# Returned rows of the second choices loaded from ScalarE's queue, those of the first choices from the sync engine

## The reference

```
x = x + _L0_ffn_ref(_layernorm(x), ...)      # top 2 of 8, silu gate
x = x + _L1_xattn_ref(ctx, ctx, _layernorm(x), mask, ...)
x = x + _L1_ffn_ref(_layernorm(x), ...)
x = x + _L2_xattn_ref(_layernorm(x), ctx, ...)
x = x + _L2_ffn_ref(_layernorm(x), ...)      # top 2 of 8, gelu
x = x + _L3_xattn_ref(_layernorm(x), ctx, ctx, ...)
x = x + _L3_ffn_ref(_layernorm(x), ...)      # top 2 of 8, relu
...
top_vals, top_idx = top_k(gate_logits, 2)
w = softmax(top_vals)
out = sum over both choices of w * expert(x)
```

## Time and profile before

| | us |
|---|---|
| median of 3 runs | 1276.0 |
| lowest and highest | 1274.1, 1277.46 |
| span of the profiled execution | 1241.1 |
| busy PE, DVE, ACT, POOL in it | 1028.2, 756.0, 658.9, 670.2 |

### The profile page before, as it was taken

One profiled execution on the slowest core, in us unless ns is written; L12 is line 12 of the kernel. 1 busy time (PEld: TensorE's weight loads), 2 busy tenths in 40 slices (PEclk: granted clock), 3 DMA queues, 4 the chain that ended last, 5 costly groups with the idle time before them and its releaser, 6 DMA issues.

```text
span 1241.1 us, 22522 instructions
## 1 busy us (share of the span) xinstructions
PE 1028.2 (83%) x6547; PEld 793.3 (64%) x6547; DVE 756.0 (61%) x2570; ACT 658.9 (53%) x2366; POOL 670.2 (54%) x1163
## 2 busy tenths in 40 slices
PE   3984999847899977986999998397699999966993
PEld 3874788734555547774677765386467776645993
DVE  4367254587878776247676687532776676754443
ACT  2225233337888952446887875243387888831321
POOL 5122456546666745257655565647475555655452
PEclk9775899977999995998999999599789999975998
DMA  3422446684920021420000000166300000014566
GB/s 60 4 27 89 131 155 208 202 145 164 389 84 2 2 69 35 136 78 1 19 1 18 18 2 18 41 178 186 96 18 2 1 1 2 2 35 124 172 203 196
DMA packets 132377, 102.82 MB, mean 83 GB/s; under 512 B 34651, under 2 KB 113939, under 8 KB 132256
## 3 DMA queue, kind: packets, MB, share of 16 engines
q1 hardware_dynamic: 121360, 82.38, 24.1%
q0 software_dynamic: 8448, 17.20, 4.2%
q10 hardware_dynamic: 2448, 1.80, 0.6%
HBM read 64.98 MB, written 36.36 MB: 82 GB/s over the span
## 4 chain that ended last, share of the span: by engine, by line
PE 53%; DVE 18%; issue 8%; POOL 8%; ACT 7%; DMA 5%; SPq 1%; DVEq 0%; ACTq 0%; POOLq 0%
PE ps L2645 5%; PE ps L2826 4%; PE ps L2647 4%; PE ps L2646 4%; PE ps L2840 4%; PE ps L2705 3%; ACT ex L1377 3%; DMA xr<-xr_d,src_i 2%; PE ps L2720 2%; POOL yq_d L884 2%; PE ps L2854 2%; POOL pp L1050 2%; PE ps L3318 2%; PE ps L3137 2%; ACT ex L1263 2%
## 5 line engine op out<-in xcount | busy, mean ns | idle before, releaser
L1050 POOL TENSOR_TENSOR pp<-ex,rc 128x256 f32<-128x256 f32 x384 | 236.1, 615 | 202.9 <-DVE rc L2178 144.9
L1263 ACT ACTIVATE ex<-ps,nmx 128x154 f32<-128x154 f32 x512 | 193.9, 391 | 70.5 <-DVE nmx L2173 69.2
L2173 DVE TENSOR_REDUCE nmx<-ps 128x2 f32<-128x308 f32 x256 | 119.4, 469 | 62.3 <-PE ps L2647 61.9
L884 POOL DMA_INDIRECT yq_d<-yq,ids_q x78 | 74.7, 957 | 75.4 <-DVE yq L1908 56.4
L2826 PEld LDWEIGHTS ps<-ident,pp 128*128 128x128 f32 x640 | 74.0, 142 | 57.5 <-POOL pp L1051 49.9
L1377 ACT ACTIVATE ex<-ps,nmx 128x154 f32<-128x154 f32 x256 | 97.4, 393 | 22.9 <-DVE nmx L2038 22.5
L2645 PE MATMUL ps<-kp,q_s 128*128 128x308 f32 x256 | 96.5, 377 | 15.1 <-ACT ex L1263 8.1
L1051 POOL TENSOR_TENSOR pp<-ex,rc 128x52 f32<-128x52 f32 x384 | 105.9, 276 | 0.0
L1263 ACT ACTIVATION_READ_ACCUMULATOR ex<-ps,nmx 128x1 f32 x512 | 105.0, 205 | 0.0
L2826 PE MATMUL ps<-ident,pp 128*128 128x128 f32 x640 | 100.5, 281 | 4.7 <-POOL pp L1051 4.7
L854 POOL TENSOR_TENSOR ln_r<-ln_v,mhalf 128x4 f32<-128x4 f32 x32 | 34.5, 1079 | 88.3 <-DVE ln_v L1659 76.8
(11 more groups left out here) (441 smaller groups left out, 2806.4 us busy)
## 6 DMA issues: line engine op xcount, KB each, us to landing
w_r<-in_L_ffn_W SPq DMA_DIRECT2D x69, 256.0 KB, 3.5
xq_d<-blankq SPq DMA_DIRECT2D x4, 4160.0 KB, 24.5
w_q<-in_L_ffn_W SPq DMA_DIRECT2D x46, 256.0 KB, 3.4
w_q<-in_L_ffn_w SPq DMA_DIRECT2D x46, 128.0 KB, 2.7
xq<-xq_d SPq DMA_DIRECT2D x22, 130.0 KB, 2.2
w_s<-in_L_ffn_W SPq DMA_DIRECT2D x8, 256.0 KB, 7.0
w_e<-in_L_ffn_W SPq DMA_DIRECT2D x8, 256.0 KB, 4.9
acc<-yq_d SPq DMA_DIRECT2D x8, 256.0 KB, 4.5
```

The source lines that it names most:

```text
L884: pool.indirect_dma_start(yq_d[:, :], bass.IndirectOffsetOnAxis(ap=ids_q[:, c:c + 1], axis=0), yq[k % NY][:, h, :], None).then_inc(q_out[k ...
L1050: pool.tensor_tensor(pp[st % 2][:, m % 4, 2 * j:2 * j + 2, :], w[:, :, 0:P], r.broadcast_to([P, 2, P]), ALU.mult)
L1263: ins = act.activation(ex[:, tt % NEX, j, :], ps[:, tt % 3, j * SK:(j + 1) * SK], ACT.Exp, bias=nmx8[:, tt % 8, j:j + 1], accum_out=sm8[:, ...
L2173: dve.tensor_reduce(nmx8[:, tt % 8, :], ps[:, tt % 3, 0:2 * SK].rearrange("p (h s) -> p h s", h=2), AX.X, ALU.max, negate=True).then_inc(n ...
```

## The change

The loads of the first choices stay on SP. Those of the second choices are issued by ScalarE: at entry A behind its four key copies; at entry B between products 7 and 8 of `preps(1, ...)`; at entry C after the last run of layer 3. ScalarE waits for the same semaphores of the scatters ahead of them. Each consumer waits for the same counts as before.

```diff
@@ region(l), SP @@
                 for b in range(B):
-                    for c, into in enumerate((acc, y_other)):
-                        sp.dma_start(into[:, bsl(b)].rearrange("p (k d) -> p k d", k=TB),
-                                     yq_d[c * B * S + b * S:c * B * S + (b + 1) * S, :].rearrange("(k p) d -> p k d", p=P)).then_inc(y_in[b], 16)
+                    sp.dma_start(acc[:, bsl(b)].rearrange("p (k d) -> p k d", k=TB), yq_d[b * S:(b + 1) * S, :].rearrange("(k p) d -> p k d", p=P)).then_inc(y_in[b], 16)
@@ sorted_runs(), SP @@
                 for b in range(B):
-                    for c, into in enumerate((acc, y_second)):
-                        sp.dma_start(into[:, bsl(b)].rearrange("p (k d) -> p k d", k=TB),
-                                     yr_d[FRONT + c * B * S + b * S:FRONT + c * B * S + (b + 1) * S, :].rearrange("(k p) d -> p k d", p=P)).then_inc(y_in[b], 16)
+                    sp.dma_start(acc[:, bsl(b)].rearrange("p (k d) -> p k d", k=TB),
+                                 yr_d[FRONT + b * S:FRONT + (b + 1) * S, :].rearrange("(k p) d -> p k d", p=P)).then_inc(y_in[b], 16)
@@ ScalarE @@
+            def second_loads(l):
+
+                for u in range(NX):
+                    act.wait_ge(*sent(l, max(k for k in range(NRUN) if k % NX == u)))
+                for b in range(B):
+                    act.dma_start(y_other[:, bsl(b)].rearrange("p (k d) -> p k d", k=TB),
+                                  yq_d[B * S + b * S:B * S + (b + 1) * S, :].rearrange("(k p) d -> p k d", p=P)).then_inc(y_in[b], 16)
@@ region(l), ScalarE, after the last run @@
+                if l == 3:
+                    second_loads(3)
@@ heads(l), ScalarE @@
-                preps(1, 0, PREPS)
+                preps(1, 0, 8)
+                if l == 3:
+                    second_loads(2)
+                preps(1, 8, PREPS)
                 turned_x(0)
@@ heads1(), ScalarE @@
                 for g in range(2):
                     prep1(g, 0)
                     prep1(g, 1)
+                for u in range(2):
+                    act.wait_ge(s_out[u], 16 * blocks(2, NRUN - 1 - (NRUN - 1 - u) % 2))
+                for b in range(B):
+                    act.dma_start(y_second[:, bsl(b)].rearrange("p (k d) -> p k d", k=TB),
+                                  yr_d[FRONT + B * S + b * S:FRONT + B * S + (b + 1) * S, :].rearrange("(k p) d -> p k d", p=P)).then_inc(y_in[b], 16)
                 for b in range(B):
                     second_share(b)
```

## The result

The changed kernel is slower: 1289.53 us median against 1276.62 us, ratio 1.0075 with a 95% interval of 1.0046 to 1.0103, that is +9.6 us (+5.9 to +13.1). (The two medians alone give 1.0101, +12.9 us; the ratio on record is taken from all fast runs of both kernels, and its interval holds that too.) Measured once more in another sitting (a sitting is one set of kernels run beside the kernel before) it was 1.0097 (1.0066 to 1.0128). The prediction, 1277.7 us and a range up to 1281.0, was too low by the greater part of the effect.

A forecast was written before the change was run, and what follows sets the result against it. VectorE's work was taken to set the pace from layer 0 to 1, a PSUM ring at layer 3's entry, the loads at the end. +0.3 + 2.2 - 0.8 = +1.7 on 1276.0 gave 1277.7 us, range 1273.5 to 1281.0.

The forecast's parts named there:

- the price of entry A: Layer 0 to layer 1: late rows nearly hidden by slack; +0.3 us, bounds 0 and +1.0.
- rival 3: Layer 0 to 1: blanks ahead leave late rows a quarter of the rate; +2.6 there, total +4.0, 1280.0 us; chance 0.13.
- two of its own signs of being wrong: Profile after would refute it if ScalarE issues take over 1 us, or VectorE or GpSimd waits for `y_second`.
- A first load lands 3.2 us after its issue: Layer 0 to 1: landing time of 3.2 us, read at the kernel's end, used for ScalarE's late loads.
- The rate: 312 GB/s to be shared by halves: Layer 0 to 1: late rows and blanks halve 312 GB/s, so 262 kB take 1.7 us.
- the rival's deciding point, a quarter of 312: Layer 0 to 1: at a quarter of the rate, 3.4 us a load, the slowdown decides the verdict; total +4.0.
- Entry B: Layer 2's feed-forward to layer 3: four issues hold ScalarE between copies, delaying `vr`; +2.2 us, bounds +1.2 and +5.6.
- Rival 2: Layer 2 to 3: issues of both queues share a backlog, ScalarE held 5.6 us; total +5.1, 1281.1 us; chance 0.10.
- Entry C: Layer 3's feed-forward to the output: loads start sooner, last sum 0.8 us earlier; -0.8, bounds 0 and -2.3.
- Rival 4: At the end, the second queue doubles the feed, gain 2.3 us; total -1.2; chance 0.22 shared with another rival.
- Slower had 0.16: Whole kernel: chance of a measurably slower result, 0.10 + 0.05 from two rivals and 0.01 for spread.
- The time outside the span: Whole kernel: median 1276.0 stands 34.9 us above the profiled span of 1241.1, taken as untouched by the change.

The follow-up runs named there:

- A alone: Second-choice loads moved to ScalarE only from layer 0 to layer 1, against the kernel before: ratio 1.0064 (1.0038 to 1.0091), +8.2 us.
- B alone: Second-choice loads moved to ScalarE only from layer 2 to layer 3, against the kernel before: ratio 1.0038 (1.0011 to 1.0066), +4.9 us.

## Why the prediction was wrong, point by point

**The failed step is the price of entry A**, +0.3, with a bound of +1.0. It measured +6.9 and +8.6 in the two traces of the changed kernel (25.43 and 27.11 against 18.5), +7.6 with A alone, and +8.2 us by the ratio. The mechanism was named, as rival 3 (blanks ahead of the late rows), and the issue at 269.48, 4.2 us behind SP's first load, came as forecast (262.3 against 257.96, 4.3). ScalarE issues of over 1 us and waits for `y_second` were two of its own signs of being wrong. Two of its terms failed:

- "A first load lands 3.2 us after its issue", whatever SP has in flight. That row was of a set of engines that moved nothing just before (0 GB/s from 1227 to 1228). The first late row landed after 11.7 us with the blanks ahead; with none ahead the shortest was 3.0.
- The rate: 312 GB/s to be shared by halves. In that window the loads still had the engines. With the blanks under way they move 126 to 159 GB/s at full shares, so 1548 KB hold them for 10 to 13 us, and even the rival's deciding point, a quarter of 312, was kinder to the first load than what happened. The row that would have told this is one that I did not weigh: in the trace of before, the same blanks took 14.1 us to land (issue, count, size, median us to landing):

```profile
xs_d<-blank SPq DMA_DIRECT2D x1, 1548.0 KB, 14.1
```

At equal turns the first late load, 262 kB, would have had to let about as many bytes of blanks pass, some 0.5 MB or 3 to 4 us at 126 to 159 GB/s (an estimate from those windows). With A alone it landed 1.4 us before the end of 1548 KB of them (281.41 against 282.8). So it stood behind almost all of the blanks. Why the two queues do not share by halves there, no view here shows; that stays open.

**Entry B**, +2.2. The mechanism was right: four issues among the copies, no cover, `vr` later by as much (+2.0 where nothing else comes in). Left out was the lower granted clock that followed PE's stand in two of three traces, worth 0.8 to 1.0 more. Rival 2, long issues because SP issues at the same time, did not come, but its condition did not either: at B SP's last issue ended 4.1 us before ScalarE's first (916.34 against 920.44), and four took 2.06 us. Where both queues issued together, four took 2.12 us at the end, 2.13 at B with all three entries, and 2.62 behind product 1 with B alone: never the 5.6 of the rival. At A ScalarE's issues did take 1.3 us each, with the blanks in flight; there ScalarE had nothing else to do.

**Entry C**, -0.8. It measured -0.5 (10.97 against 11.50). The direction was right and the size nearly. By the Trainium skill (*DMA: Bandwidth & Descriptors*, section *Issuing engines are not separate DMA queues*), which says that issuing from several engines saves only the time to issue, it would have been about 0.4; the traces agree with that better than with my figure. Rival 4, a doubled feed, is wrong.

**The sum.** 6.9 + 2.8 - 0.3 = 9.4 us from the stretches of the trace after, against 9.6 (5.9 to 13.1) by the ratio; of its second trace 8.6 + 2.0 - 0.5 = 10.1, against 12.1 (8.2 to 15.9). The parts run alone add to 1.011, which lies inside the second measurement of the whole and just above the interval of the first; their own intervals are wide enough for that.

**The chances.** Slower had 0.16 and rival 3 within it 0.05. It had been priced as marginal on a rate taken from the wrong kind of transfer; with the blanks' own landing time I would now call it the likeliest case.

**The time outside the span** was taken as 34.9 us; it is 1.8. This did not enter the difference.

## What to carry to other kernels

Moving a load to another engine's queue also takes it out of the order of the old one: ask what the old queue issues next, and price the moved load, as a worst case that came true here, as waiting for those bytes, at the rate of that kind of transfer and not at that of loads. Put issues where the new engine stands idle and early enough (here there were such gaps of 4.8 and 2.7 us; with both the stretches were as before and no loss was to be told), not among copies that another engine waits for. Check too that what the issues wait for has come by then. And where the rows are already limited by the DMA engines, as at the end here, a second queue gives only the few tenths by which they start sooner.

## What the runs showed that I had not expected

- Writes of blank rows to the table in HBM (rows of 516 bytes, from one source in SBUF) hold the DMA engines at a busy share of 1.23 to 1.30 and move 121 to 159 GB/s, with the late loads already issued behind them; loads of rows of 512 bytes move about 300 at 0.9 to 1.2. Whether the row length or the direction makes the difference was not tested.
- Four loads issued from ScalarE 2.2 to 5.2 us behind 1548 KB of SP's blanks landed with nearly the same latency, 11.7 to 12.3 us.
- An issue from ScalarE takes 0.52 us like one from SP, 1.3 with the blanks in flight.
- A stand of PE of 1.7 to 2.0 us was followed by the lower clock level in two traces of three.
- The same kernel has medians from 1243.6 to 1289.7 us in different sittings; only ratios within one sitting say anything of a change of this size.
